# A transformer layer in fp32r splits: a wait ahead of GpSimd's sums, its sums in another order, and down products in two passes

## The reference, cut to what matters

```python
x = layernorm(x + attention(x, Wq_sem, Wk_sem, Wq_geo, Wk_geo, Wv, Wo, logit_scale))   # x: 4 x 1024 x 512
# second half, for all 4096 tokens:
h = fwht(x * SU_ug) / 64                       # Hadamard over 512
up, gate = h @ W_up.T * (Wscale_ug[:2048] * 64), h @ W_gate.T * (Wscale_ug[2048:] * 64)
h = fwht(silu(gate) * up * SU_dp) / 64         # Hadamard over 2048
y = h @ W_down.T * (Wscale_dp * 64)
out = layernorm(x + y)
```

## Time and profile before

| | |
|---|---|
| median of 3 runs | 1555.66 us (1555.15 to 1556.52) |
| profiled execution, its own time | 1557.91 us |
| its span | 1556.1 us |
| TensorE matmul busy | 1522.9 us, 98% of the span |
| VectorE busy | 1035.8 us, 67% |
| ScalarE busy | 625.6 us, 40% |
| GpSimd busy | 466.1 us, 30% |
| TensorE's granted clock, mean | 0.998 |

### The profile page before, as it was taken

One profiled execution on the slowest core, in us unless ns is written; L12 is line 12 of the kernel. 1 busy time (PEld: TensorE's weight loads), 2 busy tenths in 40 slices (PEclk: granted clock), 3 DMA queues, 4 the chain that ended last, 5 costly groups with the idle time before them and its releaser, 6 DMA issues.

```text
span 1556.1 us, 26452 instructions
## 1 busy us (share of the span) xinstructions
PE 1522.9 (98%) x10152; PEld 1365.6 (88%) x10152; DVE 1035.8 (67%) x1790; ACT 625.6 (40%) x1289; POOL 466.1 (30%) x580
## 2 busy tenths in 40 slices
PE   6999999999999999999999999999999999999998
PEld 5977978888887888899999999999999999999997
DVE  6876786687678986864575576475566457557545
ACT  4163255236227665533333333333343334333322
POOL 5465456447438434500300130030030031003001
PEclk9999999999999999999999999999999999999999
DMA  7031122122122796677668668677767867766862
GB/s 283 1 108 76 35 82 102 35 82 102 64 77 93 286 380 256 245 263 282 231 243 290 236 211 292 226 243 255 269 225 236 292 216 255 277 231 220 282 225 95
DMA packets 92060, 307.44 MB, mean 198 GB/s; under 512 B 9888, under 2 KB 10272, under 8 KB 90144
## 3 DMA queue, kind: packets, MB, share of 16 engines
q1 hardware_dynamic: 90928, 301.54, 54.9%
q10 hardware_dynamic: 1008, 4.20, 0.7%
HBM read 255.37 MB, written 50.33 MB: 196 GB/s over the span
## 4 chain that ended last, share of the span: by engine, by line
PE 63%; DVE 5%; ACT 1%; issue 1%; POOL 1%; POOLq 0%; DVEq 0%; ACTq 0%
PE ff_bank_b L2058 16%; PE ff_bank_a L2058 11%; PE ff_bank_c L2058 11%; PE ff_acc L2085 7%; PE ff_acc L2086 7%; PE ff_acc L2078 7%; DVE ff_d_lo L1775 2%; PE ff_x_ps L2009 1%; PE ff_x_ps L2029 1%; ACT at_union L601 1%; DVE ff_h_lo L1794 1%; DVE ff_c L1826 0%; PE ff_x_ps L2017 0%; PE ff_x_ps L2018 0%; DVE ff_ring L1770 0%
## 5 line engine op out<-in xcount | busy, mean ns | idle before, releaser
L2058 PE MATMUL ff_bank_b<-ff_x_hi,ff_ring 128*128 128x256 f32 x1536 | 302.2, 280 | 2.5 <-DVE ff_c L1826 1.9
L2058 PEld LDWEIGHTS ff_bank_b<-ff_x_hi,ff_ring 128*128 128x128 f32 x1536 | 247.8, 188 | 3.8 <-issue 3.7
L2058 PE MATMUL ff_bank_b<-ff_x_lo,ff_ring 128*128 128x256 f32 x768 | 214.2, 279 | 0.0
L2058 PE MATMUL ff_bank_c<-ff_x_hi,ff_ring 128*128 128x256 f32 x1024 | 203.9, 282 | 0.0
L2058 PE MATMUL ff_bank_a<-ff_x_hi,ff_ring 128*128 128x256 f32 x1024 | 203.4, 282 | 0.0
L2085 PE MATMUL ff_acc<-ff_d_lo,ff_h_hi 128*128 128x512 f32 x504 | 198.0, 393 | 1.3 <-DVE ff_d_lo L1775 1.3
L2086 PE MATMUL ff_acc<-ff_d_hi,ff_h_lo 128*128 128x512 f32 x504 | 196.1, 389 | 0.0
L2058 PEld LDWEIGHTS ff_bank_a<-ff_x_hi,ff_ring 128*128 128x128 f32 x1024 | 165.3, 188 | 2.7 <-issue 0.2
L2058 PEld LDWEIGHTS ff_bank_c<-ff_x_hi,ff_ring 128*128 128x128 f32 x1024 | 165.1, 188 | 2.3 <-issue 2.3
L1822 DVE TENSOR_TENSOR ff_c<-ff_bank_b,ff_c 128x512 f32<-128x512 f32 x64 | 44.3, 692 | 175.3 <-PE ff_bank_b L2058 174.0
L2058 PEld LDWEIGHTS ff_bank_b<-ff_x_lo,ff_ring 128*128 128x128 f32 x768 | 143.7, 187 | 0.0
(11 more groups left out here) (323 smaller groups left out, 3471.2 us busy)
## 6 DMA issues: line engine op xcount, KB each, us to landing
ff_ring<-gu_scratch SPq DMA_DIRECT2D x392, 512.0 KB, 4.9
gu_scratch<-ff_ring SPq DMA_DIRECT2D x56, 512.0 KB, 4.4
at_xt<-in_xt SPq DMA_DIRECT2D x4, 2048.0 KB, 8.4
at_xn<-in_x SPq DMA_DIRECT2D x32, 256.0 KB, 2.9
x_scratch<-at_x SPq DMA_DIRECT2D x32, 256.0 KB, 2.0
ff_raw<-in_wgu SPq DMA_DIRECT2D x8, 1024.0 KB, 7.8
at_wd_a<-in_wd SPq DMA_DIRECT2D x8, 512.0 KB, 4.7
mixed_scratch<-at_wd_a SPq DMA_DIRECT2D x8, 512.0 KB, 3.2
```

The source lines that it names most:

```text
L2058: i = pe.matmul(bank[:, m, :], r[:, a, m, c, :], b[:, k, c, :], start=(k < 3 and m == 0 and c == 0 and b is x_hi and a == 0), stop=(m == 1 ...
```

## The change

GpSimd waits for the fourth split of x of block zero before it forms the weight sums of step one. For step seven, its token sums of block one now come ahead of all four weight sums, which stood around them before. In the down products, the eight matmuls of the low half of h by the high down weights now come in one pass, in front of the wait for the low half of the down weights, and the eight of the high half of h by the low down weights after it; before, the two kinds alternated behind both waits.

```diff
             def run(close_attention):
+                pool.wait_ge(*x_lo_s.now(0, 4))
                 for p in range(1, PAIRS - 1):
                     sum_weights(p)
...
                 pair_sums(1)
-                sum_weights(PAIRS - 1, (0, 1, 2))
                 butterfly(1)
-                sum_weights(PAIRS - 1, (3,))
+                sum_weights(PAIRS - 1)
...
                 between()
                 pe.wait_ge(*h_lo_s.now(s, 2))
+                for j in range(2):
+                    for t in range(FT):
+                        k = slice(P * t, P * t + P)
+                        pe.matmul(acc[:, t, :], h_lo[q][:, j, k], d_hi[:, j, :], start=False, stop=False)
                 pe.wait_ge(*d_lo_s.now(s, 1))
                 for j in range(2):
                     for t in range(FT):
                         k = slice(P * t, P * t + P)
-                        pe.matmul(acc[:, t, :], h_hi[q][:, j, k], d_lo[:, j, :], start=False, stop=False)
-                        i = pe.matmul(acc[:, t, :], h_lo[q][:, j, k], d_hi[:, j, :], start=False, stop=last and j == 1)
+                        i = pe.matmul(acc[:, t, :], h_hi[q][:, j, k], d_lo[:, j, :], start=False, stop=last and j == 1)
                 i.then_inc(down_s.sem, 1)
```

## The result

The changed kernel took 1560.59 us (median of 10 runs, 1557.31 to 1562.55), the kernel before, beside it on the same chip, 1556.59 us (10 runs, 1555.15 to 1558.08). The ratio is 1.0023, with a 95% interval of 1.0014 to 1.0033: slower by 4.0 us of median where 2.0 us were forecast, and outside the range (1560.0). Against the forecast of 1557.7 us the miss is 2.9 us: 2.0 us of it are cost, and 0.9 us are the kernel before itself, which took 1556.59 us here and 1555.66 us in the three runs that the forecast started from. The profiled execution of the changed kernel is one of its shorter runs: 1558.07 us, span 1556.3 us, mean granted clock 0.999.

What follows compares the result with a forecast made beforehand. TensorE, busy 98% of the span, was taken as the bound: a line of matmuls with small holes. Terms −1.0 + 2.9 − 0.7 + 0.8 = +2.0 us, carried over to the 1555.66 us median, gave 1557.7 us; range 1554.7 to 1560.0.

Steps and rivals of the forecast that it cites:

- the term of −1.0 us in attention: End of attention: moving step one's sums frees a VectorE subtraction TensorE waited for; −1.0 us, bounds 0 to −1.1.
- rival (d): Opening of the second half: TensorE's clock falls, eight matmuls cost 1.7 us more on top of +2.0; 1559.4 us, chance 0.05.
- strict turns: GpSimd sums and VectorE subtractions of two SBUF tensors exclude each other for whole instructions, each turn about 1.77 us.
- (a): GpSimd's late sums cost more: step seven's second weight sum ends at 639.5, fourth sum catches another subtraction; 1559.5 us, chance 0.20.
- Opening: Step one of the second half: three sums collide with VectorE's subtractions, so it ends 2.9 us late; bounds 0 to 4.0.
- Step two's sums: Weight sums of step two could delay an eviction that TensorE needs; bounds 0 to +0.7 us, taken as 0.
- Steps six and seven: Token sums delay step seven's weight sums, so product 49 and the fold come later; net +0.8 us, bounds −1.5 to +1.5.
- Part 3: Down products in steps one and two: waits only for the low half of the weights vanish; 1.3 − 0.6 = −0.7 us.
- Order over the banks: Down products: eight matmuls walking over four banks might run slower than alternating pairs; 0 to +3.0 us, taken as 0.
- Everything after block zero: From 659 us to the end: TensorE waits 1.9 us for evictions of step products, which the change does not touch.
- Rival (b): Opening mostly hidden because VectorE wins ties: added cost 0.5 instead of 2.9, so −0.4 us; 1555.3 us, chance 0.20.
- (c): Change closes holes in attention, down products and steps six and seven, opening free: −3.2 us; 1552.5 us, chance 0.05.

Runs made afterwards that it cites:

- e2: Kernel before with only the new order, token sums ahead of step seven's weight sums: 1556.88 us, ratio 1.0004.
- e3: Kernel before with only the two passes of the down products: 1557.81 us, ratio 1.0005.
- e5: Kernel before with attention's 32 narrow matmuls parted by six wide ones, no work added: 1555.62 us, ratio 0.9998.
- e13: Kernel before plus token sums first and the down passes, without GpSimd's new wait, narrow matmuls parted: 1556.43 us, ratio 0.9992.
- e6: Changed kernel with attention's 32 narrow matmuls parted by six wide ones: 1560.01 us, ratio 1.0018 to the kernel before.
- e11: The kernel of e6 profiled again, unchanged, to look for the clock's fall: 1557.40 us.
- e9: The kernel of e6 profiled again, unchanged, to look for the clock's fall: 1560.52 us.
- e10: The kernel of e6 profiled again, unchanged, to look for the clock's fall: 1560.28 us.
- e15: Kernel before plus GpSimd's wait and the down passes, without the new token order, narrow matmuls parted: 1558.19 us, ratio 1.0010.
- e16: Kernel before plus GpSimd's wait and token sums first, without the down passes, narrow matmuls parted: 1559.95 us, ratio 1.0015.
- e17: Kernel before plus GpSimd's wait alone, narrow matmuls parted, the same kernel as e12 run again: 1557.96 us, ratio 1.0011.
- e4: The changed kernel timed once more, unchanged, against the kernel before: 1560.60 us, ratio 1.0024.
- e14: Kernel before plus down passes, GpSimd waiting for the fifth lowered product, two token sums ahead of step seven's weight sums, narrow matmuls parted: 1555.09 us, ratio 0.9985.
- e1: Kernel before with only GpSimd's wait for four splits of x: 1558.07 us, ratio 1.0010.
- e7: Kernel before plus down passes and an earlier GpSimd wait, for the fifth lowered product, token sums in the old order: 1555.02 us, ratio 0.9991.
- e12: Kernel before plus GpSimd's wait alone, narrow matmuls parted: 1557.69 us, ratio 1.0005.

## Why the prediction was wrong, point by point

**Two steps failed**: the term of −1.0 us in attention, and the chance of 0.05 for rival (d).

The term of −1.0 is real in the one profile that it was read from and in none of the four others without the new wait (e2, e3, e5, e13), so it is worth 0 in four of five profiles. Bounds of 0 to −1.1 were given, and the end that seldom comes was taken, because the strict turns at 508 us were held to be the rule. With 0 in its place the forecast's own terms add up to +3.0 us. The profiles bear that out: against e5's second half that of e6 is 2.86 + 0.41 = 3.3 us longer and that of e11 2.5 us, with the same length of attention's end (101.4 us).

Rival (d) was set aside with the words "Against: the holes are cut by a full product". The product does not protect: in e9, e10, e15, e16 and e17 the clock falls to about half right behind the hole, with TensorE busy for 1.5 to 1.7 us of the 3.6 us before. Its price was near (+1.7 forecast, though eight matmuls at 0.2 us more are 1.6; 1.8 measured), its chance was not. Seven of the changed kernel's ten runs are below 0.999, and all seven took 1559.72 us or more. The range stopped at 1560.0 because it took (a) and (d) one at a time. That these seven fell in the opening is argued from the kernels with attention parted: of the two profiles of the changed kernel as it is, its own has no fall, and e4's, at 1560.18 us, has its fall in attention, where the kernel before falls too.

The Trainium skill's page "TensorE: Matmul & The Clock Gate", section "What's actually happening", which stood beside (d), says that an idle array is throttled to half speed. The 0.51 of e9 agrees as to the level. The array was not idle but thinly occupied, and that such a stretch is enough is what the traces add.

**The sum came out partly by luck.** +2.0 us were forecast, and 2.0 to 2.3 us are measured between runs at 0.999. Against the profile before, with its chance wait of 1.0 us, +2 us is right; against a kernel before without it, the second halves say 2.5 to 3.3 us. The comparison at 0.999 is also likely to be kind to the changed kernel: its profiled runs at 0.999 all have a short start (48 matmuls in 7.06 to 7.47 us), while kernels without the hole are at 0.999 with 7.99 us (e14) and 8.48 us (e13) too. The terms:

- Attention: −1.0 forecast, 0 to −0.1 in every comparison but that with the profile before.
- Opening: +2.9 forecast, 2.66 measured (2.61 in e1). The mechanism is as described, turns of 1.78 and 1.76 us; the wait is 2.08 us where 2.0 were worked out. One detail was not: at 506.23 VectorE's pair took 1.28 us and GpSimd's sum 2.42, so there VectorE kept its place and GpSimd waited, and strict turns are not general. The Trainium skill's page "SBUF — State Buffer", section "Who interferes with whom", lets the order of issue decide. The traces here can't show that order: GpSimd's recorded start is 0.04 us ahead of VectorE's in the profile before and in e5 alike, and the outcomes are opposite.
- Step two's sums: taken as 0 of 0 to +0.7. It is 0.4 us in this profile, from 2.66 to 3.06, given back by step three (2.45); e11, the same second half, has no such hole. The chain of waits shows an eviction held by a subtraction:

```profile
537.71 1.71 DVE ff_ring L1770
539.41 0.61 DVE ff_c L1826
540.02 0.14 issue
540.16 1.65 PE ff_bank_b L2058 x12
```

- Steps six and seven: +0.8 forecast, 2.91 − 2.48 = +0.4 measured. T, the end of the second weight sum, was to be 638.7; it is 636.52 + 1.62 = 638.1 on the clock of after, 638.6 on that of before. Product 49 starts after 1.55 us of waiting, against "over 1 us".
- Part 3: −0.7 forecast, −0.2 through block zero in e3 and +0.1 at the end, which is nothing beside the 0.4 us that two profiles can differ by. The three waits at L2085 vanish as I said, but TensorE is early then and meets VectorE one step on. I had counted the waits and not who stands behind them.
- Order over the banks: 0 of 0 to +3 taken. From block one to the end e3 loses 0.26 us on before, and e5, which has the old order, loses 0.20: the order costs less than 0.1 us over the 1008 matmuls. This was the widest bound, and it was empty.
- Everything after block zero: nothing forecast, about 0.2 us measured. e5 has the same 0.2 us without any part of the change, so it belongs to the profile before that all are compared with.

Rival (b) is refuted by the 2.08 us wait, (c) by the 1.55 us wait. Rival (a) has the nearest time (1559.5) for a reason that did not come: T is 638.6, not 639.5, and the fourth sum, at 527.25 us, lengthens one subtraction by 0.1 us, not by 1.1.

**What stays open** is what fixes the place of the clock's beat in a run, and so why the share of runs that fall differs between series of the same kernel (1 of 10, 4 of 11). It is also open why the falls are more frequent with the new token order; the hole of 1.6 us at 641 was never seen to bring one, but only profiled runs can show that. And how the falls of the changed kernel's own runs divide between attention and the opening was not seen. The mean clock of a run cannot count its falls: in every profiled run the granted clock is also at its lower level in the last 2.6 to 4.9 us of the span. e9, at 0.997, has that tail and the one fall in the opening and nothing else; e7, at 0.998, has the tail alone; e3, at 0.996, has two falls and the tail. So a run at 0.998 may have no fall at all, and "below 0.999" counts falls only roughly.

## What to carry to other kernels

A wait that stands once in one profile may be that execution's: look for it in a second profile before a gain is booked on it. A hole in TensorE's line has two prices, its length and the clock that it may cost behind it; where a change opens a hole of 2 us, put both into the range together, even when the hole stands between full products. A wait that keeps GpSimd out of VectorE's way has to send its work to a stretch where VectorE reads PSUM: the same sums cost 2.5 us of TensorE behind the fourth split and nothing that e7 shows behind the fifth lowered product. And when the median of a kernel moves by more than its profile explains, sort the runs by granted clock first, and then ask what else the sorting selects.

## What the runs showed of the hardware

- The clock falls to about half for some 3.4 us behind a hole of 2.08 us, at a cost of 1.8 us (e17 against e12), in some executions only. Of the profiled runs with that hole, all five whose first 48 matmuls took 8.14 to 8.27 us fell, none of the six with 7.06 to 7.47 us did, nor did e4 with 8.42 us and its hole 1 us later.
- The falls keep to a beat of the clock: counted from where the trace's record of the clock begins, the five in the opening start at 508.59 us, while the holes end 508.3 to 508.7 us behind that point.
- The first matmuls of the program run at 213 ns in place of 112 ns, for 3 to 6 us depending on the run. The profile's views read a granted clock of 1.00 there, but the trace has no record of the clock before the spacing changes: the 48 of them take 7.06 to 8.48 us, a spread of 1.4 us in a run's length.
- A GpSimd sum of two 128x512 fp32 SBUF tensors and VectorE subtractions of the same size do not always take turns: in 15 of 20 profiles VectorE did two in 1.28 us while the sum took 2.42 to 2.48 us, in five the sum went first in 1.3 us.
- Much of the spread of this kernel's times goes with the clock: at 0.999 the runs of before have a mean of 1555.94 us and at 0.998 of 1557.01 in one series, 1555.44 and 1558.09 in another. Parting 32 narrow matmuls with wide ones, with no work added or taken away, brought 10 of 11 runs to 0.999, against 13 of 32 beside it.
